# When GpSimd sends the rows of two tiles to their experts' slots: behind the even pass, or inside the odd pass that follows

## What is computed

```python
x = L0_attn_x                                    # (2, 2048, 256) float32, 16 heads of 16
x = _layernorm(x + attention(x), axis=-1)        # j <= i and j >= i - 64
logits = x @ Wr.T
expert_idx = argmax(softmax(logits))             # one of 8 for each token
for e in range(8):
    mask = (expert_idx == e)[:, None]
    inter = inter + mask * gelu(x @ W1[e] + b1[e])
y = inter @ Wo + bo + x
out = _layernorm(x + ffn_layernorm(y) * gamma + beta, axis=-1)
```

## Time and profile before

| | |
|---|---|
| median of 3 runs | 573.9 us (573.85 to 574.31) |
| span of the profiled execution, first to last instruction | 569.7 us |
| attention passes at full pace, about | 80 to 320 us of the span |
| turn between the stages | 320 to 345 us |
| expert stage | 345 to 570 us |

### The profile page before, as it was taken

The page is one execution under the profiler, slowest core; times in us unless marked ns, Lnnn a source line. Parts: engine busy times, 40 slices in busy tenths (PEclk is TensorE's granted clock), DMA queues, the critical chain, the costliest instruction groups (busy, mean ns, idle before and its releaser), DMA issues. The chain is left out here.

```text
span 569.7 us, 24810 instructions
## 1 busy us (share of the span) xinstructions
PE 505.2 (89%) x8591; PEld 444.1 (78%) x8591; DVE 413.9 (73%) x1100; ACT 354.5 (62%) x800; POOL 320.2 (56%) x570
## 2 busy tenths in 40 slices
PE   4599899989999999999977549999999999999980
PEld 3478788878787888888865439999999999998870
DVE  3746777787787977778766535888888888886443
ACT  2455667757677677776766327666666677664550
POOL 7702244535454454544455523888888888885433
PEclk9899899999999999999999659999999999999996
DMA  9597676676767887767662021333322222221000
GB/s 204 147 201 216 153 211 184 184 218 179 212 174 205 221 227 205 205 187 210 174 180 72 20 75 40 95 96 104 84 70 76 73 81 67 78 67 50 25 10 7
DMA packets 95048, 75.34 MB, mean 132 GB/s; under 512 B 37190, under 2 KB 88527, under 8 KB 94930
## 3 DMA queue, kind: packets, MB, share of 16 engines
q1 hardware_dynamic: 91570, 65.31, 43.6%
q0 software_dynamic: 3264, 8.41, 4.3%
q10 hardware_dynamic: 96, 0.04, 0.0%
HBM read 43.63 MB, written 23.62 MB: 118 GB/s over the span
## 5 line engine op out<-in xcount | busy, mean ns | idle before, releaser
L1416 PE MATMUL ps<-v_even,w_hi 128*128 128x128 f16 (+1 forms) x1280 | 170.5, 215 | 1.8 <-issue 1.1
L1416 PE MATMUL ps<-v_even,w_lo 128*128 128x128 f16 (+1 forms) x640 | 132.2, 214 | 0.0
L837 ACT ACTIVATE probs<-ps,b1T 128x128 f32<-128x128 f32 (+1 forms) x320 | 87.0, 360 | 72.5 <-PE ps L1416 54.1
L1398 PE MATMUL ps<-wo_hi,ks 128*128 128x256 f16 x576 | 128.6, 273 | 1.0 <-DVE ks L1087 1.0
L1416 PEld LDWEIGHTS ps<-v_even,w_hi 128*128 x1280 | 120.9, 98 | 7.4 <-issue 3.7
L870 DVE TENSOR_REDUCE mx<-ps 128x4 bf16<-128x512 f32 x128 | 83.4, 683 | 20.9 <-PE ps L1195 13.6
L629 POOL CAST att_hi<-att 128x256 f16<-128x256 f32 x32 | 12.7, 396 | 120.9 <-DVE att L928 120.9
L1398 PE MATMUL ps<-wo_lo,ks 128*128 128x256 f16 x288 | 78.5, 273 | 0.0
L734 ACT ACTIVATE probs<-ps 128x512 f32<-128x512 f32 x128 | 69.8, 611 | 9.9 <-PE ps L1221 7.5
L1244 PE MATMUL ps<-v_even,probs 128*64 128x17 f32 x1024 | 71.6, 210 | 3.8 <-issue 3.0
L1244 PE MATMUL ps<-v_odd,probs 128*64 128x17 f32 x1024 | 71.8, 210 | 3.5 <-issue 3.4
(11 more groups left out here) (225 smaller groups left out, 1254.1 us busy)
## 6 DMA issues: line engine op xcount, KB each, us to landing
qk_s<-qk_hi SPq DMA_DIRECT2D x64, 128.0 KB, 2.7
w_in<-in_L_ffn_W_dram SPq DMA_DIRECT2D x32, 256.0 KB, 3.0
v_odd<-slots SPq DMA_DIRECT2D x64, 128.0 KB
qs<-qk_s SPq DMA_DIRECT2D x16, 384.0 KB
ks<-qk_s SPq DMA_DIRECT2D x16, 384.0 KB, 4.9
ks<-qk_s SPq DMA_DIRECT2D x32, 144.0 KB, 3.7
v_even<-v_odd SPq DMA_DIRECT2D x63, 68.0 KB, 3.4
qk_s<-qk_lo SPq DMA_DIRECT2D x32, 128.0 KB, 3.3
```

The costliest lines, as they stand in the source:

```text
L837: last = nc.scalar.activation(g[1 - p][:, ic, n * width:(n + 1) * width], ps_h[1 - p][:, half, col + n * width:col + (n + 1) * width], ACT ...
L1398: ins = mm(ps_y[p], h[p][hs][:, ic, :], wo[ws][:, ic, :], start=n == 0, stop=n == 3 * IC - 1)
L1416: up_ins = mm(ps_h[1 - p][:, half, col + m * width:col + (m + 1) * width], weights(ws, owners[m], k, ic), sT[1 - p][ss][:, k, at], start=k ...
```

## The change

The sends of tiles `it-4` and `it-3` at the end of even passes are gone. In an odd pass the same two tiles, now `it-5` and `it-4`, are sent between the addition of the projection bias to the input (L624) and the split of the attention output (L629). Ahead of the first of them stands one new wait: the first half of the value products of tile `it-1`, the ones that TensorE does in this very pass, must be done. Where there is no tile `it-1` any more (pass 33) that wait is absent. The last pair is sent in pass 34 as before. The number of sends stays 32.

```diff
+            def send_rows(first):
+                for n in (first, first + 1):
+                    apart(pool)
+                    wait(pool, number_done, n - ROWS + 1)
+                    pool.wait_ge(slot_done, n // 2 + 1)
+                    pool.wait_ge(x1_done, n + 1)
+                    nc.gpsimd.indirect_dma_start(
+                        out=slots, out_offset=bass.IndirectOffsetOnAxis(ap=slot_of[n // 2 % 2][:, n % 2:n % 2 + 1], axis=0),
+                        in_=row[n % ROWS][:, :], in_offset=None, bounds_check=SLOTS - 1, oob_is_err=False)\
+                        .then_inc(disp_st[n % ROWS], 16)
...
                     nc.gpsimd.tensor_tensor(xin[n % XRING], xin[n % XRING], bp[:, :], ALU.add).then_inc(xrb_done, 1)
+
+                if it % 2 == 1 and a_tile(it - 5):
+                    if a_tile(it - 1):
+                        pool.wait_ge(pv_done, CC * (it - 1) + 1)
+                    send_rows(it - 5)
                 n = it - 1
...
-                for n in (it - 4, it - 3) if it % 2 == 0 else ():
-                    if a_tile(n):
...
+                if it == LAST:
+                    send_rows(it - 4)
```

## The result

The changed kernel takes 587.33 us (median of 4 runs, 586.61 to 589.15) where the kernel before took 574.11 us beside it (4 runs, 573.85 to 577.14). The ratio is 1.0249 with a 95% interval of 1.0192 to 1.0305: **slower by 2.5%, about 13 us**. The forecast of 577.0 us had the sign, and the time lies outside its range. The experiments ran in three groups, each beside its own runs of the kernel before, whose medians were 571.44, 574.78 and 573.71 us.)

A forecast was written before the change was run, and what follows sets the result against it. TensorE, busy 505 of 569.7 us, was taken to bound the attention stage. Span 569.7 + 3.6 (12 pairs at +0.3) - 0.5 = 572.8 us, plus 4.2 to the median: 577 us; own range 575 to 580, 80% range 569 to 581.5.

The forecast's parts named there:

- The hold itself: While GpSimd runs two sends, finished TensorE work is seen late, until about 3.1 us behind the first send's start.
- The predicted signs: In the profile: odd-pass value products take 1.1 us without a stop; intervals that held sends take 8.1 us, not 8.8 to 9.0.
- The rival that took from the Trainium skill: Sends never touch TensorE, so today's 0.8 us stays and GpSimd's queue adds 14 x 0.6 = +8.4: 582 us; chance 0.05.
- What the sends cost before: End of even passes: a pair of sends loses 0.7 to 0.9 us, taken as 0.8, against an undisturbed 8.12 us.
- The 0.27 us that I gave the rank matmuls: Difference in when value products start, 5.21 against 4.94 us, subtracted from 8.39 to get the undisturbed interval of 8.12 us.
- Start of the sends: Odd pass: first send 1.0 us (0.75 to 1.2) behind the value products' first half; GpSimd free at +3.33.
- First cost, GpSimd's queue: Odd pass: the attention output's split waits behind the sends, `att_lo` done at +4.53 not +3.4; TensorE waits 0.7 us (0.4 to 0.9).
- Second cost, the late completions: Odd pass: maxima seen at +3.95, so the transposed scores' second half starts at +5.9, not +4.9: 1.0 us lost.
- the case that it is held: Rival: the value products' completion is seen late, 1.4 us lost a pair, 12 x 0.6 = +7.2 us, 581 us; chance 0.09.
- upper case: Odd pass: value products seen 2.3 us behind the send, `att_lo` at +5.2, TensorE loses 1.4 us.
- the allowance for bad pairs: 0.1 us added for pairs of sends that fall badly, making the net +0.3 us in each of 12 pairs.
- The last two pairs: Passes 29 and 31, without query and key products: TensorE waits for `att_lo` anyway; the change gives 0.25 us each, -0.5 together.

The follow-up runs named there:

- the longer fill: Kernel before, sends at their old place, plus a GpSimd memset of 128 x 3600 numbers in odd passes behind the changed kernel's wait: 575.99 us, ratio 1.0034.
- plain sends: Changed kernel with plain GpSimd transfers of the same rows to fixed places instead of indirect ones: 577.05 us, ratio 0.9901.
- rows through SyncE: Kernel before without GpSimd's sends; SyncE writes the same rows by plain transfers to fixed places behind the same passes: 571.46 us, ratio 0.9963.

## Why the prediction was right and wrong

*The hold itself: right, and finer now.* An indirect transfer of GpSimd delays what others see of TensorE. Results due from about 0.3 us behind its start are held, until 1.3 to 1.7 us behind it for a single one and mostly until 2.8 to 3.4 us behind the first of a pair. The predicted signs are there: the stop in the value products at the turn is gone (0.90 us from first to last start of the first half; 1.15 to 1.99 before, at all but one pair), and the intervals that held the sends take 8.13 us against a predicted 8.1. The rival that took from the Trainium skill ("SBUF — State Buffer", section "Who interferes with whom": TensorE and ScalarE never wait on anyone) that the sends don't touch TensorE would have left them at 8.8 to 9.0, so the trace disagrees with that reading. The section speaks of SBUF ports, and no run here shows whether a port has a part in the hold.

*What the sends cost before: 0.8 us forecast, 0.79 measured at that place, and 0.23 overlooked in quiet passes.* The 0.27 us that I gave the rank matmuls weren't theirs. Where sends are absent, intervals with and without ranks take 8.16 and 8.13 us: the ranks cost 0.03. The other 0.23 us of the 8.39 are gone where no sends stand, so they were a knock-on of the sends in the previous pass. The figure for the undisturbed interval came out right by luck, and the whole cost of a quiet pair was 8.39 + 8.80 - 16.29 = 0.9 us. Over all 12 pairs at full pace it was 9.01 + 8.68 - 16.29 = 1.4.

*Start of the sends: nearly right.* +0.82 us behind the first half, for +1.0; GpSimd free at 247.10 - 243.95 = +3.15, for +3.33.

*First cost, GpSimd's queue: not where the time went.* It was put at 0.7 us. GpSimd was idle for 1.27 us between the sends and the split, waiting for VectorE, so the queue bound nothing here. With the queue alone filled (the longer fill) it cost 0.05 to 0.5 in quiet passes.

*Second cost, the late completions: the step that failed.* Its part on the maxima held: ScalarE began to write them at +4.12, forecast +3.95. But I let the second half of the value products slip through the hold, because it was due only 0.35 us behind the send, and put the case that it is held at 0.09. With the earlier start of the sends it was due 0.53 us behind it, and at 12 of the 14 pairs in odd passes it was announced 2.8 to 3.3 us behind the send (at the first pair, where it was due at 0.38, at 1.34; at the last at 2.08). My own had a result due at 0.37 and seen at 2.30; I called it the exception and it was the rule. Even my upper case was too short: it released the value products at 2.3 us behind the send, and they came at 2.8 or later. So `att_lo` came at +5.58 and not at +4.53 or +5.2, and an interval that begins in an odd pass mostly took 10.1 to 10.8 us, not 9.4. The first pair shows the step by itself: where the value products did slip through, TensorE had no wait for `att_lo` and the interval took 88.05 - 78.33 = 9.72 us. The loss is 2.0 us for a quiet pair against an undisturbed pass, where I had 1.0. Net of the cost that went away it is 1.0 to 1.1 us a pair, forecast 0.3 with the allowance for bad pairs; over the 12 pairs at full pace +12.4 us for +3.6. I had written that if the range failed, it would be through pairs that fall badly; it failed through nearly every pair.

*The last two pairs: wrong in sign.* I forecast a gain of 0.5 us from passes 29 and 31, since TensorE waits for `att_lo` there anyway. They cost 4.8. Without the query and key products TensorE reaches its transposes right behind the maxima and has nothing that covers the hold: it waited 3.59 us in one stretch, and the clock's lower level accounts for most of the rest of that interval. My forecast had no term for the clock, in pass 27 either. How often that clock step comes can't be told from one profiled execution. The runs without a profile lie at or above the profiled one, so it isn't a freak of that one; the kernels with the longer fill and with plain sends show an interval of 11.6 us one pass earlier, so the hold need not be all that brings such intervals about. In the kernel before the clock falls too, but later, from about 313 us on (0.56 to 0.59 over 4 us, behind a wait of 1.57 us for `att_lo`).

*The sum.* The forecast span was 572.8 us. The full-pace passes account for +8.8 of the difference to 584.9, the last two pairs for +5.3, what lies behind them for +1.9 and what lies ahead for -3.8.

Still open: what inside an indirect transfer holds the completions. The experiments show that it is neither the bytes nor GpSimd being busy, and that a plain transfer doesn't do it. Which of the indirect form's own steps does it wasn't tried. Open too is why the kernels without a hold (plain sends, rows through SyncE) don't take the 17 us less that 12 pairs at 1.4 us make; waits for keys and stretches at the lower clock stand where the gain should be.

## What to carry to other kernels

When work moves to a place where an engine is "idle anyway", ask what it does to the others while it runs: here 2 us of GpSimd time, fully covered on its own engine, delayed three results of TensorE by 1.4 to 2.8 us. A result that was seen late once near a suspect instruction is a bound that the forecast must price at full weight, at the new place too; and a quiet pass of the same trace, with nothing of the suspect near, is the only honest baseline. If a disturbance is short when single and long when doubled, spread it: at the old place one send a pass was faster than either kernel here (0.987, and 0.995 and 0.993 in longer series), at the new place it wasn't faster than the kernel before (1.010).

## What the runs showed of the hardware

- An indirect transfer issued by GpSimd (1.05 us of its time) holds most of what other engines see of TensorE until 1.3 to 1.7 us behind its start; two of them 1.36 us apart, mostly until 2.8 to 3.4. With 8 numbers a row instead of 257 it is the same. Two plain transfers from GpSimd (1.15 us for both) hold nothing: none of 479 completions was late, against 41 of 472.
- In the trace such a hold never appears on TensorE's own rows, whose ends are modelled. It shows as late starts of those who wait, with the releaser "remote" or a matmul that had ended long before.
- The kernels without a hold were not faster by what it cost: TensorE waited for key loads there (7.9 us with the rows through SyncE, 6.5 with GpSimd's plain sends, 0.2 in the changed kernel), and some intervals ran in part at the lower clock.
- In the changed kernel TensorE's granted clock stood at 0.50 from 305 us on, inside a wait of 3.59 us, until about 322, and from 288 to 291 us, 1 us behind the end of a wait of 1.53 us; another wait of 1.53 us, at 118 us, left it at 1.00.
